# Gelu of a group's expert products: one activation of 4096 columns in the first tile, in place of two of 2048 in the third and the first

## The reference, cut to what matters

```python
xn = batch_norm(x)                       # over all tokens
sim = einsum(q(xn), keys)                # 8 heads, 2 halves, 32 keys each
s, i = top_k(sim, 8)                     # per half
scores, pk = top_k(sx[..., :, None] + sy[..., None, :], 8)   # pairs of the two halves
o = einsum('bnd,bnhkd->bnhk', inputs, key_in[idx])
o = gelu(o, approximate=False) * softmax(scores)
return einsum('bnhk,bnhkd->bnd', o, key_out[idx])
```

## Time and profile before

| | |
|---|---|
| median of 3 runs | 1811.86 us (1811.05 to 1820.54) |
| profiled execution, own time | 1817.61 us |
| its span, first to last instruction | 1815.9 us |
| granted TensorE clock, mean | 0.958 |
| busy: PE, DVE | 1536.1 us, 1481.7 us |
| busy: ACT, POOL | 1268.6 us, 1332.3 us |

### The profile page before, as it was taken

One profiled execution on the slowest core, in us unless ns is written; L12 is line 12 of the kernel. 1 busy time (PEld: TensorE's weight loads), 2 busy tenths in 40 slices (PEclk: granted clock), 3 DMA queues, 4 the chain that ended last, 5 costly groups with the idle time before them and its releaser, 6 DMA issues.

```text
span 1815.9 us, 37722 instructions
## 1 busy us (share of the span) xinstructions
PE 1536.1 (85%) x11712; PEld 1091.8 (60%) x11712; DVE 1481.7 (82%) x3720; ACT 1268.6 (70%) x1741; POOL 1332.3 (73%) x1579
## 2 busy tenths in 40 slices
PE   3899999999999999768887888878878788887877
PEld 2455555555556666346666766666666666666656
DVE  3668888788888887159899988989889898898988
ACT  1156666666666666558888878888888888788885
POOL 1045555555555555569999999999999999999993
PEclk9689999999999999879999998999999999999999
DMA  5334444443444442100000000000000000000000
GB/s 141 76 81 98 99 97 95 101 96 95 103 103 103 99 99 56 43 29 1 19 18 1 19 18 18 0 18 18 1 18 18 11 8 18 18 0 18 13 6 7
DMA packets 73406, 85.14 MB, mean 47 GB/s; under 512 B 9856, under 2 KB 63616, under 8 KB 68608
## 3 DMA queue, kind: packets, MB, share of 16 engines
q1 hardware_dynamic: 73312, 84.08, 19.7%
HBM read 58.10 MB, written 25.95 MB: 46 GB/s over the span
## 4 chain that ended last, share of the span: by engine, by line
POOL 24%; issue 19%; DVE 7%; ACT 5%; PE 1%; POOLq 0%; DVEq 0%; ACTq 0%; SPq 0%
POOL SUM L751 24%; DVE W L944 4%; ACT E L852 3%; ACT L786 1%; DVE M8Y L888 0%; PE WT L1012 0%; DVE SMALL L888 0%; DVE SMALL L905 0%; ACT GE L785 0%; DVE CT L927 0%; ACT SIM L779 0%; ACT BNT L794 0%; PE MB L979 0%; DVE Z L911 0%; PE E L967 0%
## 5 line engine op out<-in xcount | busy, mean ns | idle before, releaser
L751 POOL TENSOR_TENSOR SUM<-SIM 128x1024 f32<-128x1024 f32 x512 | 959.9, 1912 | 39.8 <-DVE W L944 36.1
L944 DVE SCALAR_TENSOR_TENSOR W<-SUM,SMALL,E 128x1024 f32<-128x1024 f32 x512 | 646.1, 1280 | 86.2 <-ACT E L852 82.1
L852 ACT ACTIVATE E<-SUM,NB 128x1024 f32<-128x1024 f32 x512 | 567.4, 1118 | 136.1 <-DVE W L944 121.6
L1012 PE MATMUL WT<-idf,W 128*128 128x128 f32 x4096 | 554.3, 285 | 104.2 <-DVE CT L927 53.5
L1012 PEld LDWEIGHTS WT<-idf,W 128*128 128x128 f32 x4096 | 476.3, 147 | 274.8 <-DVE W L944 143.0
L264 POOL TENSOR_SCALAR_AFFINE_SELECT PT<-PT 128x128 f32<-128x128 f32 (+1 forms) x1024 | 336.4, 353 | 323.4 <-ACT PT L354 287.2
L409 DVE TENSOR_REDUCE mx<-SX 128x2 f32<-128x512 f32 x256 | 175.4, 685 | 102.7 <-PE SX L492 102.0
L411 DVE TENSOR_REDUCE mx<-SY 128x2 f32<-128x768 f32 x256 | 242.7, 948 | 7.7 <-PE SY L492 7.3
L354 ACT ACTIVATE PT<-TX 128x512 f32<-128x512 f32 x256 | 152.8, 597 | 102.2 <-PE TX L519 100.9
L356 ACT ACTIVATE PT<-TY 128x768 f32<-128x768 f32 x256 | 207.0, 808 | 2.0 <-PE TY L519 0.8
L488 PE MATMUL SY<-K,Q 72*128 72x384 bf16 x512 | 164.0, 343 | 15.6 <-DVE mx L411 14.9
(11 more groups left out here) (111 smaller groups left out, 1671.1 us busy)
## 6 DMA issues: line engine op xcount, KB each, us to landing
K<-k_parts SPq DMA_DIRECT2D x96, 192.0 KB
Q<-q_parts SPq DMA_DIRECT2D x288, 64.0 KB
q_parts<-qp SPq DMA_DIRECT2D x16, 384.0 KB, 2.4
k_parts<-kp SPq DMA_DIRECT2D x16, 384.0 KB, 2.4
xin<-in_x SPq DMA_DIRECT2D x16, 256.0 KB, 3.1
xres<-in_x SPq DMA_DIRECT2D x16, 256.0 KB, 9.0
x<-X SPq DMA_DIRECT2D x16, 256.0 KB, 2.3
x2T<-X2T SPq DMA_DIRECT2D x16, 256.0 KB, 2.1
```

The lines of the kernel that those rows point to most:

```text
L751: return eng.tensor_tensor(SUM[(q * FH + h) % RING][:, :].rearrange("p (i j) -> p i j", i=NK), sx, sy, ALU.add)
L852: nc.scalar.activation(E[h % 2][:, :], SUM[(k * FH + h) % RING][:, :], ACT.Exp, bias=NB[q][:, h:h + 1]).then_inc(S["exp_ready"], 1)
L944: nc.vector.scalar_tensor_tensor(out=W[h % WRING][:, :], in0=SUM[(k * FH + h) % RING][:, :], scalar=TOP[q][:, h, TOPK - 1:TOPK], in1=E[h % ...
L1012: o = pe.matmul(WT[:, e, :], W[h % WRING][:, e * P:(e + 1) * P], ident[:, :], is_transpose=True, start=(h == 0 and e % 4 == 0), stop=(h == ...
```

## The change

ScalarE does the Gelu of all eight products of a group in one activation, after head 3 of the group's own first tile; the one in the third tile is gone, with its two table loads. The semaphore `gelu_ready` now counts one per group. VectorE's ranking order in the third tile goes from `BURST` to `EVEN`.

```diff
-        def gelus(g, b, half):
+        def gelus(g, b):
 
-            act.wait_ge(S["expert_copied"], g * BLK + (half + 1) * 4)
-            o = GE[b][:, 4 * half:4 * half + 4, :].rearrange("p e n -> p (e n)")
+            act.wait_ge(S["expert_copied"], (g + 1) * BLK)
+            o = GE[b][:, :, :].rearrange("p e n -> p (e n)")
             nc.scalar.activation(o, o, ACT.Gelu).then_inc(S["gelu_ready"], 1)
             nc.scalar.preload_act_table_set("natural_log_exp_and_others")
...
-        act.sem_inc(S["gelu_ready"], 2)
+        act.sem_inc(S["gelu_ready"], 1)
...
-                    if (k, h) == (2, 3) and more:
-                        gelus(g + 1, 1 - b, 0)
                     if (k, h) == (0, 3) and real:
-                        gelus(g, b, 1)
+                        gelus(g, b)
...
-            dve.wait_ge(S["gelu_ready"], (g + 1) * 2)
+            dve.wait_ge(S["gelu_ready"], g + 1)
...
-                        for part in (EVEN if k % 2 else BURST)[h]:
+                        for part in (EVEN if k else BURST)[h]:
```

## The result

The changed kernel takes 1820.7 us (median of 22 runs, 1813.9 to 1830.9) against 1816.3 of the kernel before in its 22 (1811.1 to 1820.5, but for one slow run of 1967.8 that is left out of the ratio): ratio 1.0033, 95% interval 1.0021 to 1.0045. By the ratio that is 6 us more (4 to 8), by the two medians 4.4. It is inside the half per cent that counts as no change here, but off zero. The forecast was +8.2 us, most likely "no change".

What follows compares the result with a forecast made beforehand. VectorE's pace, not GpSimd's, was taken to bound the kernel. Third tile -24.4, first tile's Gelu +25.6, a CT wait gone -1.0 and TensorE's clock +8.0 make +8.2 us on 1811.9: 1820 us, range 1808 to 1830.

Steps and rivals of the forecast that it cites:

- The bound: Second stage: VectorE sets the pace at 62.84 us a group, against GpSimd's 60.0.
- The third tile: Without its Gelu and with the spread order it takes 14.64 instead of 16.27 us: 24.4 us saved in 15 groups.
- The first tile: Its doubled Gelu takes 3.62 us, 1.71 more, none of it hidden: +25.6 us in 15 groups, bounds 23.8 to 28.7.
- the two row estimates: The 4096-column Gelu's time, reckoned from column costs of 0.80 and 0.876 ns: 3.56 and 3.71 us.
- The fourth tile: CT's wait for TensorE that belongs to the third tile's stop goes: some 1.0 us less.
- The clock: TensorE, idle 4.7 instead of 2.99 us, runs at half clock afterwards; CT waits in second tiles: +8.0 us, bounds 0 to +18.5.
- 12.5 less 4.5: CT's waits behind first tiles' stops: 10 x 1.1 + 5 x 0.3 = 12.5 us expected, less 4.5 us already there.
- The price rule: CT's added wait in the second tile is half of TensorE's added slow time, less a slack of about 1.35 us.
- The sum: Whole kernel: -24.4 + 25.6 - 1.0 + 8.0 = +8.2 us, from 1811.9 to 1820 us.
- TensorE keeps up: Rival, chance 0.28: the longer idle makes no more slow stretches than now; +1.2 us, 1813 us.
- Nearly every stop long: Slower rival, chance 0.16: a long slow stretch of TensorE follows nearly every first-tile stop; +19.7 us, 1831.6 us.
- ScalarE's total counts: Faster rival, chance 0.08: ScalarE's total, 41.6 us less, decides and VectorE gets the longer Gelu hidden; 1787 us.

Runs made afterwards that it cites:

- burst_third: The changed kernel with VectorE's ranking order in the third tile put back to the burst; ratio 1.0081 to the kernel before.
- half_columns: The changed kernel with its one Gelu over the first 2048 of 4096 columns, the other four products' Gelu left out; ratio 0.9838 to the kernel before.
- fill5_after: The changed kernel with five filling products, results unused, on TensorE in each first tile's idle time; ratio 0.9986 to the kernel before.

## Why the prediction was right

- **The bound.** VectorE's pace, not GpSimd's: right. GpSimd's wait for VectorE rose with the kernel's time, 36.1 to 41.6 us.
- **The third tile.** 24.4 us forecast, 24.5 measured. burst_third splits it: 1.21 a tile for the wait and the rest of the stop, 0.42 for the burst order.
- **The first tile.** The Gelu was put at 3.62 between ends of 3.50 and 3.83; it takes 3.623. (The middle of the two row estimates, 3.56 and 3.71, is rather 3.63; that would add 0.2 us.) The wait behind the burst was to be 2.86, and is 2.88. Forecast +25.6, measured +26.1; half_columns takes 26.3 back. The Trainium skill's 0.833 ns a column (page "ScalarE: Activation LUTs", section "What ACT_TABLE_LOAD costs") is what the rows give: (3.623 - 1.913) / 2048 = 0.835.
- **The fourth tile.** Forecast -1.0, measured -2.5: without a stop in the third tile, all fourth tiles are at 14.56 to 14.63. The forecast went by the listed waits of CT alone.
- **The clock.** Forecast +8.0, measured +5.8 in the second tiles. The mechanism was right: the clock fell at 15 of 15 stops, and filling TensorE takes the whole cost away. Both terms of "12.5 less 4.5" were too large. The 12.5 took all 15 stops to be 4.7 us long. Nine were, and six of these nine had a long slow stretch (still 4.3 to 6.1 us after TensorE resumed), two in three as estimated, with waits of 0.67 to 1.61, mean 1.17; the other three had a wait of 0.2 or none. The six shorter stops, where the loop turns and in the last group, had waits of 0.3 at most. At four of these six places the kernel before, too, had stops of only 1.5 to 2.3 us. All in all CT waited 8.6 us behind first tiles' stops. The 4.5 held 1.2 us of the kernel's very last CT, which stands behind no stop and waits as long in both kernels (VectorE's timeline of the kernel before):

```profile
1809.56 1.22 DVE L927 TENSOR_TENSOR CT<-WT,GE 128x1024 f32<-128x1024 f32 x1 [1.19 <-PE WT L1012]
```

Only 3.2 us of before stood behind first tiles' stops, so 5.3 us of waiting were added, and CT's waits in all, forecast at "over 10 us", are 9.6. What I had not thought of is where the clock falls. At 11 of the 15 stops, all nine long ones among them, it fell while TensorE was still idle; at four it fell 0.4 to 1.1 us after work had resumed. The price rule, half of the slow time behind the stop less 1.35, gives the waits of the nine long stops to 0.2 us.
- **The sum.** +8.2 forecast, +6 (4 to 8) measured. The small misses of the fourth tile and of the clock both point down; the first tiles took 0.5 more. That the absolute 1820 was met by 1820.7 is in part luck: the forecast stood on a median of three runs, 1811.9, and the kernel before is at 1816.3 in 22.
- **The rivals.** "TensorE keeps up" fell: fill5_after is 8.5 us faster. "Nearly every stop long" fell, six of 15. "ScalarE's total counts" fell clearest: ScalarE's busy time went down by 38 us in the change and up by 74 us or more in the four-Gelu kernels, and the times went the other way or stayed. The rule of the Trainium skill, page "ScalarE: Activation LUTs", section "Table sets: the hidden batching unit", to batch calls by table set does save ScalarE the loads. Each is 1.283 us here, less than half of the 2.7 us that the section puts on one. In this kernel ScalarE's total is not what is paid.

## What to carry to other kernels

In this kernel a stop of ScalarE (two table loads and a Gelu) made VectorE wait for what it exceeded the work queued beside it, not for its length. The stops of 3.67, 4.52 and 6.23 us, with Gelus of 1024, 2048 and 4096 columns, gave waits of 0.30, 1.15 and 2.88: each time the stop less some 3.4 us. The cover is not free either: the burst that fills the stop costs 0.45 a tile by burst_third. So four short stops, with twice the loads of two, did no worse than two or one. Once the batch norm was moved as well, the bias rows span 981.2 us with four, 984.8 with two and 989.5 with one, in one execution each; the intervals of the ratios overlap. Before merging two such operations, compare each one's overhang, and look at what the stop idles further down: here TensorE, once starved, cost again when it resumed, at half its clock. And what stands right behind the long instruction is on the path; move it to where that engine waits.

## What the runs showed of the hardware

- The fall to half clock can begin within the idle time and end well after it. Of the nine stops of 4.70 us in the kernel after, three left 2.9 to 3.2 us of slow work and six left 4.3 to 6.1; what decides between them no run shows. The runs of the kernel after spread over 17 us. The four longest (1826.6 to 1830.9) have a mean granted clock of 0.949 to 0.951, the four shortest (1813.9 to 1819.0) of 0.955 to 0.958, so time and clock go together; that the one makes the other was not tested. The Trainium skill, page "TensorE: Matmul & The Clock Gate", section "Part 1: The HAM clock gate", has the slow clock begin after idle time and end after busy time; the trace agrees at all 15 stops here, with the slow clock beginning up to 2.5 us before TensorE resumed at 11 and up to 1.1 us after at four. In the kernel before it fell at 16 of 30 stops, of 1.5 to 3.0 us.
- Throwaway products on TensorE, five of 384 columns per group, made the kernel 8.5 us faster. Seven made it no faster: the output copy waited for them, 6.8 us in all.
- First tiles at which the twelve-group loop turns (groups 4, 6, 8, 10, 12) take 1.7 to 2.0 us more than the others in both kernels, 20.4 to 20.7 against 18.66 in the kernel after. The profile puts that wait down to ScalarE, whose exponential was long done. With filling products some turns took up to 2 us more again. I did not find the cause, and no run was made for it.
